# A Mamba-2 block between two FFNs: the out projection from rounded halves, with the loop's weight halves made on GpSimd

## The chip, the cores and the metric

One NeuronCore of a Trainium2 chip runs the whole kernel. The metric is the device time of one execution in microseconds, lower is better. The engines are PE (TensorE), DVE (VectorE), ACT (ScalarE), POOL (GpSimd) and SP (SyncE, which here only issues DMAs). Each runs its own instructions in order; semaphores join them.

## What is computed

The input is x, 2048 tokens by 256 channels, float32. Layernorm and half an FFN are added, then a Mamba-2 mixer on the layernorm of that, then half an FFN again. The mixer, cut to what matters:

```python
proj = hidden_states @ in_proj_w           # gate (4096), x, B, C, dt
hbc = silu(conv4(proj_xBC) + conv_b)       # causal, 4 taps, per channel
dt = softplus(dt + dt_bias); dA = dt * -exp(A_log); cum = cumsum(dA, chunk)
scores = (C @ B.T) * exp(cum_i - cum_j) * dt_j          # j <= i
Y_diag = scores @ x
states = sum_l exp(cum_end - cum_l) * dt_l * B_l x_l
new = exp(cum_end) * prev + states         # scan over chunks, prev starts at 0
Y_off = (C @ prev) * exp(cum)
hidden = (Y_diag + Y_off + D * x) * silu(gate)
hidden = hidden * rsqrt(mean(hidden**2) + EPS) * norm_w
out = hidden @ out_proj_w                  # 4096 -> 256
```

There are 64 heads of 64 channels and a state of 128 per head. The kernel uses chunks of 128 tokens in place of the reference's 32, which gives the same sums.

## The kernel before

**Stages.** The prologue decodes the FFN weights, runs the first FFN in 24 ticks (`for k in range(FFN_TICKS)`) and, beside it and in the first eight slots of the loop, makes B, C, dt and the decay tables (`prep`). Then comes the mixer's loop, then the second FFN. The changed work stands in the loop, and its first weights in `prep` of the FFN's ticks.

**The loop.** The 64 heads are 32 pairs (a pair is 128 channels), taken in 8 groups of GP = 4 pairs; the 2048 tokens are NT = 4 tiles of 512. A piece of work v is one pair of one tile. In a group of SLOTS = 16 pieces the tile goes slowest: v % 4 is the pair, v // 4 % 4 the tile t. Each engine runs `for s in range(-8, 128)`; slot s handles different pieces in different stages, and u below is s % 16.

- PE in slot s: states(s+2), turn_x(s+3), diag(s+1), proj_g(s+8), proj_x(s+8), out_proj(s), off(s+2). The two projections are six products each of rounded halves (`split_matmul`: high x high, high x low, low x high, for two blocks of 128 rows); out_proj is two plain float32 products (128 x 128 weights, 512 columns), each two records in the trace. off is four float32 products, one a chunk, with the state before that chunk as the stationary side; for t = 0 the first state is `zero_state`, a tile of zeros.
- DVE in slot s: conv_tap(s+7) in three steps, with scan(s+2) of one chunk between them (two instructions a chunk, one per head), times_dt and to_chunk_end(s+3), the fourth scan, skip_path(s+1) (adds D*x, writes `hid`), masked(s+2) (the decay times CB, 128 x 1024, both operands in SBUF), scale_off(s+2) (the off products times `e_row`, 512 columns), and in slots with s % 4 == 3 add_out(s).
- ACT in slot s: square(s), relus(s+3) (eight pieces of exp's argument), evac_g and evac_x(s+8), exps(s+3). In slots with s % 4 == 0 the silus of four pieces, seven of the eight before relus, come first, and the evacuations and the eighth silu too. The weight work stands at the end of a slot: `split_g_hi` at u = 6 and 8, `split_x_hi` at u = 6 to 9, `scale_wo` at u = 13 to 15 and 0.
- POOL in slot s: add_squares(s), sum_halos(s+8) in some, gate(s+1) (`hid` times silu of the gate), then `split_g_lo` at u = 6 and 8 and `split_x_lo` at u = 6 to 9.
- SP in slot s: load_cum(s+5), load_e(s+4), then weight loads of the next group. load_cum(v) waits for relus(v-2), load_e(v) for scale_off(v-2). `e_row` has two buffers. Each is a row of 512 read for 128 or 64 partitions from DRAM, two loads a piece.

**What the order hangs on.** out_proj(v) waits for gate(v) and the scaled weights. proj_g(v) waits for the gate weights of its half of the group (`gw_lo_done`, pair_of(v)//2 + 1), proj_x(v) for its pair's. off(v) waits for the scans and for skip_path(v-1), which frees the PSUM bank. scale_off(v) waits for off(v) and `e_row`, diag(v) for scale_off(v). skip_path(v) waits for diag(v) and, since `hid` has two buffers, for out_proj(v-2). ACT's square(v) waits for gate(v) and for add_squares(v-1).

## Time and profile before

| | us |
|---|---|
| median of 3 runs (1499.59 to 1504.02) | 1502.01 |
| profiled execution, its own time | 1504.3 |
| its span, first to last instruction | 1502.2 |
| mean granted TensorE clock | 0.968 of full |
| PE, DVE, ACT, POOL busy | 1384.0, 1182.2, 1037.0, 547.7 |
| loop in its regular part | about 354 to 1317 us |

The trace is that of one execution. A busy time counts an instruction from its start to its end; matmuls of a stream overlap, so that the distance between two starts, and not the busy time of one, is what a product costs. In the timeline instructions of one line that follow each other are merged, with their count. A timeline row has the start in us, the busy time in us, engine, line, operation, tiles written and read with their sizes, and the count. The bracket at the end of a row is the idle time of that engine before it and whom it waited for. SPq is the queue of SP's DMA issues; the view of one tile gives, for the DMA issues in a stretch, the shortest, median and longest time from issue to landing. The loop's rows stand from the third group of pairs, whose slot u = 1 starts its projections at 614.03; the seven groups repeat to 0.02 us.

### The profile page before, as it was taken

How to read it: one execution, taken by the hardware profiler on the slowest of the kernel's cores; microseconds unless marked ns; L12 is line 12 of the kernel's file. 1: busy time of each engine (PE TensorE's matmuls, PEld its weight loads, DVE VectorE, ACT ScalarE, POOL GpSimd, SP SyncE). 2: the span in 40 equal slices, each digit the busy share in tenths (PEclk: the TensorE clock that was granted, in tenths of full speed). 3: DMA queues.
4: the chain of work that ended last, by engine and by line, in shares of the span. 5: the costliest groups of instructions: out<-in, count | busy, mean ns of one | idle time of the engine just before them, and what ended most of it. 6: DMA issues, size and time to landing. Idle time of an engine off the chain costs nothing. (4 is left out here: it accounts for less than half of the span.)

```text
span 1502.2 us, 26126 instructions
## 1 busy us (share of the span) xinstructions
PE 1384.0 (92%) x8704; PEld 1087.0 (72%) x8704; DVE 1182.2 (79%) x2675; ACT 1037.0 (69%) x2133; POOL 547.7 (36%) x511
## 2 busy tenths in 40 slices
PE   5889977777999999999999999999999999986998
PEld 4878766555777777777777777777777777764787
DVE  5753443675999999999999999999999999996433
ACT  1124433666898888889888888988888898871332
POOL 1003211013444454445445444544544454451000
PEclk9999989888999999999999999999999999996999
DMA  5220000223434444343454534545433444324000
GB/s 125 72 88 25 15 15 14 63 50 92 117 96 108 123 111 116 101 109 104 110 130 105 114 99 103 117 112 121 114 104 92 117 118 109 97 88 182 15 14 28
DMA packets 102078, 136.35 MB, mean 91 GB/s; under 512 B 27744, under 2 KB 49856, under 8 KB 101824
## 3 DMA queue, kind: packets, MB, share of 16 engines
q1 hardware_dynamic: 99840, 132.67, 33.8%
q10 hardware_dynamic: 2112, 2.10, 0.4%
q8 instruction: 68, 1.11, 0.3%
q14 instruction: 58, 0.48, 0.1%
HBM read 124.76 MB, written 9.96 MB: 90 GB/s over the span
## 5 line engine op out<-in xcount | busy, mean ns | idle before, releaser
L998 POOL TENSOR_TENSOR hid<-hid,sg 128x512 f32<-128x512 f32 x128 | 272.7, 2130 | 372.8 <-DVE hid L1265 371.0
L844 ACT ACTIVATE M<-cum_row,cum_table 128x128 f32<-128x128 f32 x1024 | 312.0, 390 | 0.0
L1203 DVE SCALAR_TENSOR_TENSOR xs<-psum,conv_w_sb,xs 128x509 f32<-128x509 f32 (+2 forms) x384 | 285.1, 742 | 0.4
L1598 PE MATMUL psum<-hid,wo 128*128 128x512 f32 x512 | 243.1, 597 | 9.6 <-ACT eT L755 9.3
L987 POOL TENSOR_TENSOR squares<-squares,sq 128x512 f32<-128x512 f32 x124 | 165.9, 1338 | 158.9 <-ACT sq L821 158.6
L1230 DVE TENSOR_TENSOR M<-M,CB 128x1024 f32<-128x1024 f32 x128 | 158.7, 1240 | 0.0
L1598 PEld LDWEIGHTS psum<-hid,wo 128*128 128x128 f32 x512 | 96.2, 189 | 84.6 <-issue 72.9
L1257 DVE TENSOR_TENSOR psum<-psum,e_row 128x512 f32<-128x512 f32 x128 | 89.5, 699 | 81.5 <-PE psum L1572 81.5
L1583 PE MATMUL psum<-M,xdt 128*64 128x128 f32 x2048 | 140.1, 279 | 0.9 <-DVE psum L1257 0.9
L1558 PE MATMUL psum<-xend,B_tok 128*128 128x128 f32 x1024 | 137.2, 278 | 0.0
L852 ACT ACTIVATE M<-M 128x1024 f32<-128x1024 f32 x128 | 134.5, 1051 | 0.5
L821 ACT ACTIVATE sq<-hid 128x512 f32<-128x512 f32 x124 | 77.5, 625 | 78.8 <-POOL hid L998 78.8
L858 ACT ACTIVATE xs<-psum,conv_b_sb,conv_w_sb 128x512 f32<-128x512 f32 x128 | 98.6, 770 | 46.0 <-PE psum L40 46.0
L1558 PEld LDWEIGHTS psum<-xend,B_tok 128*128 128x128 f32 x1024 | 127.1, 195 | 1.1 <-issue 1.0
L1583 PEld LDWEIGHTS psum<-M,xdt 128*64 128x64 f32 x2048 | 109.2, 136 | 22.3 <-issue 22.2
L1250 DVE SCALAR_TENSOR_TENSOR inner<-inner,decay_table,psum 128x64 f32<-128x64 f32 x512 | 118.5, 275 | 0.0
L38 PE MATMUL psum<-xT_hi,gw_hi 128*128 128x512 f32 x256 | 114.6, 448 | 2.2 <-DVE x_res L1061 1.5
L1572 PE MATMUL psum<-CT,inner 128*128 128x128 f32 x768 | 107.9, 277 | 0.0
L826 ACT ACTIVATE sg<-psum 128x512 f32<-128x512 f32 x128 | 74.7, 583 | 45.7 <-PE psum L40 38.0
L40 PE MATMUL psum<-xT_hi,gw_lo 128*128 128x512 f32 x256 | 102.1, 399 | 0.0
L38 PE MATMUL psum<-xT_hi,xw_hi 128*128 128x512 f32 x256 | 101.6, 397 | 0.0
L39 PE MATMUL psum<-xT_lo,gw_hi 128*128 128x512 f32 x256 | 101.5, 396 | 0.0
(201 smaller groups left out, 2912.4 us busy)
## 6 DMA issues: line engine op xcount, KB each, us to landing
cum_row<-cum_scratch SPq DMA_DIRECT2D x256, 256.0 KB, 4.3
e_row<-e_scratch SPq DMA_DIRECT2D x256, 128.0 KB, 3.6
xw_raw<-L_attn_in_proj_w_dram SPq DMA_DIRECT2D x32, 128.0 KB, 2.9
wo_raw<-L_attn_out_proj_w_dram SPq DMA_DIRECT2D x32, 128.0 KB, 3.0
gw_raw<-L_attn_in_proj_w_dram SPq DMA_DIRECT2D x16, 256.0 KB, 6.6
x_res<-_attn_hidden_states_dram ACTq DMA_DIRECT2D x4, 512.0 KB, 9.8
x_scratch<-x_res SPq DMA_DIRECT2D x4, 512.0 KB, 2.6
x_res<-x_scratch SPq DMA_DIRECT2D x1, 2048.0 KB, 8.8
```

The lines of the kernel that those rows point to most:

```text
L38: nc.tensor.matmul(out, l_hi, r_hi, start=start, stop=False, skip_group_check=skip)
L844: last = nc.scalar.activation(M[:, v % 3, h, c * CH:(c + 1) * CH], cum_row[:, v % 2, h, c * CH:(c + 1) * CH], ACT.Relu, bias=scalar_of(CUM ...
L852: nc.scalar.activation(M[:, v % 3], M[:, v % 3], ACT.Exp, scale=-1.0).then_inc(exp_done, 1)
L987: nc.gpsimd.tensor_tensor(squares[:, tile(t)], squares[:, tile(t)], sq[:], ALU.add).then_inc(squares_done, 1)
L998: nc.gpsimd.tensor_tensor(hid[:, v % 2, :], hid[:, v % 2, :], sg[:, v % 8, :], ALU.mult).then_inc(hid_done, 1)
L1203: nc.vector.scalar_tensor_tensor(xs[:, v % 8, shift:], psum[:, X_BANK + v % 2, 0:TT - shift], tap_of(v, step), xs[:, v % 8, shift:], ALU.m ...
L1230: nc.vector.tensor_tensor(M[:, v % 3], M[:, v % 3], cb, ALU.mult).then_inc(M_done, 1)
L1250: nc.vector.scalar_tensor_tensor(after, before, scalar_of(CHUNK_DECAY, v, chunk, h), psum[:, ST_BANK, c * P + h * HP:c * P + (h + 1) * HP] ...
L1558: last = nc.tensor.matmul(psum[:, ST_BANK, c * P:(c + 1) * P], B_tok[:, t * CPT + c, :], xend[:, v % 2, c].rearrange("p h q -> p (h q)"), ...
L1572: last = nc.tensor.matmul(psum[:, Y_BANK, c * CH:(c + 1) * CH], before.rearrange("p h q -> p (h q)"), CT[:, tok:tok + CH], start=(c == 0), ...
L1583: last = nc.tensor.matmul(psum[h * HP:(h + 1) * HP, Y_BANK, c * CH:(c + 1) * CH], xdt[:, v % 3, c, h, :], M[:, v % 3, h, c * CH:(c + 1) * CH],
L1598: last = nc.tensor.matmul(psum[:, OUT_BANK + m, :], wo[:, j, m * P:(m + 1) * P], hid[:, v % 2, :], start=(j == 0), stop=(j == GP - 1))
```

## The change

1. **Out projection.** `wo` (float32) becomes `wo_hi` and `wo_lo`, `hid` gets `hid_hi` (two buffers) and `hid_lo` (one). out_proj is now 2 x 3 products of rounded halves. POOL makes the halves of the product in `split_hid(s+1)`, right behind gate(s+1).
2. **Loop weights on POOL.** `split_x` (u = 5, 6, 7, 9), `split_g` (u = 6, 9) and `split_wo` (u = 13, 14, 15 and 1 of the next group) make the high halves by a copy and the low ones by a subtraction, all on POOL; ACT's part in the loop goes. Before the loop ACT still makes high halves, in ticks moved about.
3. **Zero state.** For t = 0, off skips the first chunk, scale_off leaves out its columns, and scan of the first chunk is one copy. `zero_state` goes.
4. **Room.** `e_row`, `xend` go from two buffers to one, `xdt` from three to two, `gw_raw` to half a group's gate weights; load_e moves from s+4 to s+3 and waits for scale_off(v-1), loads are moved to fit.

The diff, cut to its core:

```diff
@@ tiles @@
-    wo = sb("wo", [P, GP, D], F32)
+    wo_hi = sb("wo_hi", [P, GP, D], F32R)
+    wo_lo = sb("wo_lo", [P, GP, D], F32R)
-    e_row = sb("e_row", [P, 2, TT], F32)
-    xdt = sb("xdt", [P, 3, CPT, 2, HP], F32)
-    xend = sb("xend", [P, 2, CPT, 2, HP], F32)
+    e_row = sb("e_row", [P, TT], F32)
+    xdt = sb("xdt", [P, 2, CPT, 2, HP], F32)
+    xend = sb("xend", [P, CPT, 2, HP], F32)
+    hid_hi = sb("hid_hi", [P, 2, TT], F32R)
+    hid_lo = sb("hid_lo", [P, TT], F32R)
+    G_TICKS = (4, 7)
+    WO_TICKS = (5, 6, 12, 15)
+    X_SLOTS = (5, 6, 7, 9)
+    G_SLOTS = (6, 9)
@@ sync @@
             def load_e(v):
-                sp.wait_ge(off_scaled, nth(v - 2))
+                sp.wait_ge(off_scaled, nth(v - 1))
...
-                if alive(s + 4):
-                    load_e(s + 4)
+                if alive(s + 3):
+                    load_e(s + 3)
...
                 if u == 4:
                     load_g_weights(2 * (g + 1))
+                if u == 7:
                     load_g_weights(2 * (g + 1) + 1)
-                if u in (7, 8):
-                    load_x_weights((g + 1) * GP + u - 5)
+                if u in (6, 7):
+                    load_x_weights((g + 1) * GP + u - 4)
-                if u in (13, 14):
-                    load_wo((g + 1) * GP + u - 11)
+                if u in (14, 15):
+                    load_wo((g + 1) * GP + u - 12)
@@ scalar, in the loop @@
-                if g < GROUPS - 1 and u in (6, 8):
-                    split_g_hi(2 * (g + 1) + u // 2 - 3)
-                if g < GROUPS - 1 and 6 <= u < 6 + GP:
-                    split_x_hi((g + 1) * GP + u - 6)
-                if g < GROUPS - 1 and u >= 13:
-                    scale_wo((g + 1) * GP + u - 13)
-                if g > 0 and u == 0:
-                    scale_wo(g * GP + GP - 1)
@@ gpsimd @@
+            def split_hid(v):
+                pool.wait_ge(hid_done, nth(v))
+                pool.wait_ge(out_done, nth(v - 2))
...
+                nc.gpsimd.tensor_copy(hid_hi[:, v % 2, :], hid[:, v % 2, :]).then_inc(hid_hi_done, 1)
+                pool.wait_ge(hid_hi_done, nth(v))
+                pool.wait_ge(out_done, nth(v - 1))
+                nc.gpsimd.tensor_tensor(hid_lo[:], hid[:, v % 2, :], hid_hi[:, v % 2, :].bitcast(F32),
+                                        ALU.subtract).then_inc(hid_lo_done, 1)
+            def split_x(p):
+                cols = slice(p % GP * P, (p % GP + 1) * P)
+                pool.wait_ge(xw_in[p % 2], (p // 2 + 1) * 16)
+                pool.wait_ge(x_proj, nth(last_of(p - GP)))
+                nc.gpsimd.tensor_copy(xw_hi[:, :, cols], xw_raw[:, p % 2]).then_inc(xw_hi_done, 1)
+                split_x_lo(p)
+            def split_g(q):
+                cols = slice(q % 2 * 2 * P, (q % 2 + 1) * 2 * P)
+                pool.wait_ge(gw_in, (q + 1) * 16)
+                pool.wait_ge(g_proj, nth(last_of(2 * q + 1 - GP)))
+                nc.gpsimd.tensor_copy(gw_hi[:, :, cols], gw_raw[:]).then_inc(gw_hi_done, 1)
+                split_g_lo(q)
+            def split_wo(p):
+                pool.wait_ge(wo_in[p % 2], (p // 2 + 1) * 16)
+                nc.gpsimd.tensor_tensor(wo_raw[:, p % 2, :], wo_raw[:, p % 2, :], norm_sb[:, p:p + 1].to_broadcast([P, D]),
+                                        ALU.mult).then_inc(wo_done, 1)
+                pool.wait_ge(out_done, nth(last_of(p - GP)))
+                pool.wait_ge(wo_done, p + 1)
+                nc.gpsimd.tensor_copy(wo_hi[:, p % GP, :], wo_raw[:, p % 2, :]).then_inc(wo_hi_done, 1)
+                split_wo_lo(p)
...
                 if alive(s + 1):
                     gate(s + 1)
+                    split_hid(s + 1)
                 g, u = divmod(s, SLOTS)
+                if g > 0 and u == 1:
+                    split_wo(g * GP + GP - 1)
                 if s < 0 or g == GROUPS - 1:
                     continue
+                if u in X_SLOTS:
+                    split_x((g + 1) * GP + X_SLOTS.index(u))
+                if u in G_SLOTS:
+                    split_g(2 * (g + 1) + G_SLOTS.index(u))
+                if u >= 13:
+                    split_wo((g + 1) * GP + u - 13)
@@ vector @@
+                if chunk == 0:
+                    nc.vector.tensor_copy(inner[:, v % 2, 0].rearrange("p h q -> p (h q)"),
+                                          psum[:, ST_BANK, 0:P]).then_inc(scan_step, 1)
+                    return
...
+                cols = slice(CH if at_slot(v)[1] == 0 else 0, TT)
+                nc.vector.tensor_tensor(psum[:, Y_BANK, cols], psum[:, Y_BANK, cols], e_row[:, cols],
+                                        ALU.mult).then_inc(off_scaled, 1)
...
             def skip_path(v):
-                dve.wait_ge(out_done, nth(v - 2))
+                dve.wait_ge(hid_lo_done, nth(v - 2))
@@ tensor @@
             def off(v):
-                for c in range(CPT):
+                first = 1 if t == 0 else 0
+                for c in range(first, CPT):
...
             def out_proj(v):
-                pe.wait_ge(hid_done, nth(v))
-                pe.wait_ge(wo_done, pair_of(v) + 1)
+                pe.wait_ge(hid_hi_done, nth(v))
+                pe.wait_ge(hid_lo_done, nth(v))
+                pe.wait_ge(wo_lo_done, pair_of(v) + 1)
...
-                    last = nc.tensor.matmul(psum[:, OUT_BANK + m, :], wo[:, j, m * P:(m + 1) * P], hid[:, v % 2, :],
-                                            start=(j == 0), stop=(j == GP - 1))
+                    last = split_matmul(nc, psum[:, OUT_BANK + m, :], wo_hi[:, j, cols], wo_lo[:, j, cols],
+                                        hid_hi[:, v % 2, :], hid_lo[:], start=(j == 0), stop=(j == GP - 1))
```

## Rows read from the trace of the kernel before

**Rows 1.** Page, part 1: busy us, share of span, instructions.
```profile
PE 1384.0 (92%) x8704; PEld 1087.0 (72%) x8704; DVE 1182.2 (79%) x2675; ACT 1037.0 (69%) x2133; POOL 547.7 (36%) x511
```

**Rows 2.** Timeline, PE, first projection: u=1, u=10, next u=1.
```profile
614.03 0.50 PE L38 MATMUL psum<-xT_hi,gw_hi 128*128 128x512 f32 x1
...
687.09 0.50 PE L38 MATMUL psum<-xT_hi,gw_hi 128*128 128x512 f32 x1
...
743.80 0.50 PE L38 MATMUL psum<-xT_hi,gw_hi 128*128 128x512 f32 x1
```

**Rows 3.** Timeline, PE, slot u = 14: projections, out projection, off.
```profile
719.96 0.39 PE L38 MATMUL psum<-xT_hi,gw_hi 128*128 128x512 f32 x1
...
722.06 1.88 PE L1598 MATMUL psum<-hid,wo 128*128 128x512 f32 x4
...
723.77 0.38 PE L1572 MATMUL psum<-CT,zero_state 128*128 128x128 f32 x2
...
723.99 0.83 PE L1572 MATMUL psum<-CT,inner 128*128 128x128 f32 x6
```

**Rows 4.** Timeline, DVE, POOL, PE, scale_off of u=3 to u=4.
```profile
635.63 0.70 DVE L1257 TENSOR_TENSOR psum<-psum,e_row 128x512 f32<-128x512 f32 x1 [0.57 <-PE psum L1572]
...
636.24 1.28 DVE L1278 TENSOR_TENSOR mixed<-psum,mixed 128x512 f32<-128x512 f32 x2
...
637.43 0.15 DVE L1195 COPY halo<-psum 128x3 f32<-128x3 f32 x1
...
641.94 0.47 DVE L1250 SCALAR_TENSOR_TENSOR carry<-inner,decay_table,psum 128x64 f32<-128x64 f32 x2
...
642.32 0.75 DVE L1265 SCALAR_TENSOR_TENSOR hid<-xs,d_sb,psum 128x512 f32<-128x512 f32 x1
...
642.98 1.23 DVE L1230 TENSOR_TENSOR M<-M,CB 128x1024 f32<-128x1024 f32 x1
...
643.15 2.19 POOL L998 TENSOR_TENSOR hid<-hid,sg 128x512 f32<-128x512 f32 x1 [3.58 <-DVE hid L1265]
...
643.21 0.46 PE L1572 MATMUL psum<-CT,carry 128*128 128x128 f32 x2 [0.57 <-DVE hid L1265]
...
644.38 0.70 DVE L1257 TENSOR_TENSOR psum<-psum,e_row 128x512 f32<-128x512 f32 x1 [0.18 <-PE psum L1572]
```

**Rows 5.** POOL groups by form: busy us, mean ns; idle before.
```profile
L959 POOL TENSOR_TENSOR gw_lo<-gw_raw,gw_hi 128x512 fp32r<-128x512 f32 x14 | 18.0, 1282 | 24.9 <-ACT gw_hi L694 24.9
...
L953 POOL TENSOR_TENSOR xw_lo<-xw_raw,xw_hi 128x256 fp32r<-128x256 f32 x28 | 20.5, 732 | 0.9
...
L923 POOL MEMSET gate_idx_sb<- 128x256 int32 x1 | 0.3, 312 | 0.3 <-POOLq L1752 0.3
...
L1752 POOL MEMSET const-float32-1.0<- 128x1 f32 x1 | 0.1, 98 | 0.0
```

**Rows 6.** Timeline, POOL and DVE, end of slot u = 9.
```profile
682.65 0.74 POOL L953 TENSOR_TENSOR xw_lo<-xw_raw,xw_hi 128x256 fp32r<-128x256 f32 x1
...
682.92 1.55 DVE L1230 TENSOR_TENSOR M<-M,CB 128x1024 f32<-128x1024 f32 x1
...
683.34 2.27 POOL L987 TENSOR_TENSOR squares<-squares,sq 128x512 f32<-128x512 f32 x1
```

**Rows 7.** Timeline, SP's DMA queue, slot u = 4.
```profile
645.94 0.80 SPq L607 DMA_DIRECT2D cum_row<-cum_scratch  x2
...
646.78 1.09 SPq L615 DMA_DIRECT2D e_row<-e_scratch  x2
```

**Rows 8.** Tile e_row, issues at 614.19 and at 646.78.
```profile
DMA to landing us min/median/max: 4.8/5.1/5.3
...
DMA to landing us min/median/max: 5.8/6.3/6.9
```

**Rows 9.** Timeline, PE, out projection of slot 0.
```profile
346.76 3.75 PE L1598 MATMUL psum<-hid,wo 128*128 128x512 f32 x4 [9.34 <-ACT eT L755]
```

**Rows 10.** Timeline, PE, first off product of slot 120.
```profile
1324.58 0.46 PE L1572 MATMUL psum<-CT,carry 128*128 128x128 f32 x2 [3.29 <-DVE hid L1265]
```

More of the change, by code:

```diff
@@ L401, in macaron @@
     wo_raw = sb("wo_raw", [P, 2, D], F32)
-    wo = sb("wo", [P, GP, D], F32)
+    under, sbu = scope()
+    w_bc_raw = sbu("w_bc_raw", [P, KT, 2 * N], F32)
+    w_dt_raw = sbu("w_dt_raw", [P, KT, H], F32)
+    under.close()
+    wo_hi = sb("wo_hi", [P, GP, D], F32R)
+    wo_lo = sb("wo_lo", [P, GP, D], F32R)
     under, sb = scope()
@@ L505, in scans @@
         g, u = divmod(v, SLOTS)
-        return g * 120 + 8 * u - 2 * max(u - 12, 0) + 2 * c + h + 1
+        t = u // GP
+        earlier = g * (GP * (7 + 8 + 8 + 6)) + 8 * u - min(u, GP) - 2 * max(u - 3 * GP, 0)
+        return earlier + (max(2 * c + h, 1) if t == 0 else 2 * c + h + 1)
     def sums_before(v):
@@ L1247, in scan @@
                     else:
-                        before = zero_state[:, h, :] if t == 0 else carry[:, t % 2, j, h, :]
+                        before = carry[:, t % 2, j, h, :]
                     after = carry[:, (t + 1) % 2, j, h, :] if c == CPT - 1 else inner[:, v % 2, c, h, :]
```

144 lines of the change are left out of this document (78 added, 66 removed).

## The prediction

> **What bounds the kernel now.** I read the page's busy shares first [rows 1]: PE 92%, DVE 79%, ACT 69%, POOL 36%, over prologue, loop and second FFN together. The change touches the loop over 128 slots, so the shares of the loop decide, and more than these the distances between its slots. The first projection of a slot returns every 129.77 us for a group of 16 slots [rows 2]. Inside a group there are only two kinds of slot. Twelve are 7.95 us long and PE runs through them without a gap: six gate and six x products at 0.233 us each (nine of them take 2.10 us), then out_proj from 722.06 to 723.77, 1.71 us, then `off`, states, turn_x, diag [rows 3]. The other four follow add_out (u = 0, 4, 8, 12; u is the slot number modulo 16). There DVE is the bound: from one scale_off to the next it does add_out, three taps, the scans, times_dt, to_chunk_end, skip_path and `masked`, and PE waits 0.57 us for skip_path before `off` [rows 4]. That slot takes 8.75 us (635.63 to 644.38). u = 8 has no halo copy (0.07 less), u = 12 no fourth scan (0.38, 641.94 to 642.32) and no halo product (0.14): 12 x 7.95 + 8.75 + 8.68 + 8.23 + 8.75 = 129.8, which closes with the 129.77 seen. Take add_out's 1.19 us away (636.24 to 637.43) and DVE's own chain is 7.56 us, 0.39 under PE's. So a second bound stands close behind, and what is late on DVE by more than that stays late until the next slot that PE bounds.
>
> **The change, part by part.**
>
> *Out projection.* Now 2 float32 products, four records, 1.71 us [rows 3]. After: 6 rounded products of the projections' form, 6 x 0.233 = 1.40 us. Saved 0.31 us in a slot that PE bounds, which becomes 7.64 us; nothing in the four long ones. The second bound (7.56) is then 0.08 behind.
>
> *Zero state.* In the slots u = 14, 15, 0, 1 the first of four `off` products goes: 0.22 us (723.77 to 723.99) [rows 3]. On DVE two scans at 0.19 us of pitch each (641.94 to 642.32 [rows 4]) become one copy of 128 columns, put at 0.19, and scale_off loses 128 of 512 columns, 0.13 of its 0.70. The three PE-bound ones become 7.42 us, the long one (u = 0) 8.75 - 0.13 - 0.19 - 0.18 = 8.25.
>
> Sum of the direct savings: nine slots x 0.31 + three x 0.53 + 0.50 = 4.88 us a group, 39 us in all, if nothing else moves.
>
> *ACT* loses the loop's weight halves (ten operations a group). It isn't the bound: worth nothing. Before the loop it gets four more copies beside a PE-bound FFN: nothing.
>
> *GpSimd, price of what it gets.* A two-input operation costs 1.28 us for 512 columns, 0.73 for 256 [rows 5]. A one-input copy of such size isn't in the trace. Below, the memset: 0.31 for 256 columns, 0.098 for one, so 0.53 for 512. Above, 1.28, a two-input one. I take 0.62 for 512 and 0.40 for 256, near the memset since it reads one operand at most. [...]
>
> *The halves of the gated product.* Let T be the end of skip_path, where `masked` starts. The gate starts at T + 0.16 and takes 2.19, since `masked` reads at the same time; alone such an operation takes 1.28 [rows 4, 5]. Copy 0.62, a wait on its own semaphore 0.06, subtraction 1.28: done at T + 4.31. The out projection needs it at about T + 6.5, in the next slot. The subtraction also waits for the out projection before; that is over by T + 0.5. add_squares (1.28) is queued behind: GpSimd is free at T + 5.6 of 7.6. Hidden, and ACT's next square that waits for add_squares isn't due before T + 9. Its cover is 2 us; the GpSimd weights use it up.
>
> *The weights on GpSimd.* x: 0.40 + 0.06 + 0.73 = 1.19 us; gate: 0.62 + 0.06 + 1.28 = 1.96; out: 0.73 + 0.06 + 1.19 = 1.98, in one iteration each. One alone fits. The iterations u = 6 and u = 9 have x and gate: GpSimd ends the weights at T + 4.31 + 1.19 + 1.96 = T + 7.46.
> - From u = 9 comes the second gate half. proj_g of slot u = 10 waits for it (pair 2 of the next group). In the trace T of slot 9 is 682.92 [rows 6] and that projection starts at 687.09 [rows 2], T + 4.17; after, T + 3.86. It will find its weights at T + 7.5: PE stands still for 3.6 us. Before, ACT's half was made in slot 8, one slot earlier. Everything behind hangs on this projection (out_proj, off, scale_off), so DVE gains nothing in it either. 3.6 us in each of 7 groups: 25 us.
> - In u = 6, add_squares runs T + 7.46 to 8.75 and the next `masked` comes at T + 7.5. Such a collision is in the trace: the GpSimd subtraction ran from 682.65, `masked` came at 682.92 and took 1.55 instead of 1.22, and the add_squares behind it took 2.27 instead of 1.28 [rows 6]. Each waits for the whole of the other. Between 0 and 1.2 us lost, by a hair's breadth of the start; I take 0.6.
>
> *e_row single.* DVE frees it at the end of scale_off, and the two loads must be there for the next scale_off. SP runs in order: load_cum(s+5) stands ahead of load_e(s+3), and in slots u = 0, 4, 8, 12 its relus are late, behind seven silus. There e_row is issued at 646.78, 2.40 us after scale_off began (644.38), right behind cum_row [rows 4, 7]. The second load starts 0.5 later and lands after another 5.3 us (u = 0), 6.9 (u = 4, with two gate loads behind it) [rows 8]. Now there are two buffers and this has 16 us. After, it lands at 2.40 + 0.31 (ACT's string starts from the gate, which DVE sets, while PE's part comes 0.31 sooner) + 0.5 + 5.4 = 8.6 us after that scale_off, against a slot of 7.64. In u = 1 the string is 0.71 later rather than 0.31 (DVE saves less than PE in the zero slots), landing at 9.0 against 7.42; in u = 5, with one gate load behind instead of two, 6.1 for the last landing and 9.35 in all. So scale_off is late by 1.6 (u = 1), 1.7 (u = 5), 1.0 (u = 9), 1.0 (u = 13). DVE wins back 0.08 to 0.36 a slot until the next DVE-bound slot. Left: 1.5 + 1.4 + 0 (under the 3.6 us stall) + 0.4 = 3.3 us a group.
>
> *xdt at two, xend at one buffer.* They wait for a diag and a states that end 1.6 us or more before: nothing. SP's other loads come in the order in which their buffers free; the nearest, the second gate load, has ten microseconds.
>
> *Ends.* At 346.76 the out projection ran at the low clock, 3.75 us where the loop has 1.88 [rows 3, 9]; six products at twice 0.233 are 2.8 there, and zero products go: -1.5 us. In the last eight slots there are no projections, the slots are some 5.3 us, and GpSimd needs 2.19 + 0.16 + 1.96 + 1.28 = 5.6; the last gate has 1.96 more behind it: +2.5 us.
>
> **Sum.** A group: -4.88 + 3.6 + 0.6 + 3.3 = +2.6 us; seven groups +18.4. The first group's u = 1 has no silus ahead: -1.5. Slots 112 to 119, no weights: -2.6 + 2.1 = -0.5. Ends +1.0. Total +17.4 us. The profiled execution took 1504.3 us, its span 1502.2; the median of the three shown is 1502.0, so the same work varies by 2 us and I count from the median: 1519.4 us, 1.2% slower.
>
> **The rivals.**
> (a) *e_row isn't late.* Its landing was measured among the transfers of now; with one gate load fewer and the loads spread, the tail may fall under 4.4 us. For it: quiet slots. Against: the late ones all have cum_row ahead of e_row, and that stays. Then a group is -4.88 + 3.6 + 0.6 = -0.7, and 1502 - 5 - 2.6 + 1 = 1495.5 us: faster. It decides where e_row lands less than 7.6 us after scale_off began.
> (b) *The full gain.* e_row in time, and the gate half too, if proj_g could run without it: 1502 - 39 + 1 = 1464 us. The wait in the code speaks against it.
> (c) *GpSimd's copy costs as a two-input operation.* Then 0.66 more in each split of the product, and 1.65 in the stall at u = 10 (+11.5 us); with the out weights add_squares ends at T + 8.6 and meets `masked` in four more slots, 2.5 us a group (+17): 1548 us. It decides from a copy of about 0.9 us.
> (d) *The clock falls in the 3.6 us stall.* [...] If 3.6 us is enough, the 4.3 us of projections behind it double: +4 x 7 = 28, 1548 us. [...]
> (e) *The savings are smaller*, the second bound catching all: within the range.
>
> **How the numbers follow.** Forecast 0.55; (a) 0.17; (b) 0.06; (c) 0.13; (d) 0.05; (e) 0.04. Range: the forecast's own terms vary by 0 to 1.2 us in the collision, 1 us in each landing, 0.3 in the stall, some 12 us either way: 1507 to 1532. For 8 in 10 it must take in (a) and half of (c): 1493 to 1545. Faster or slower by over 0.3% (4.5 us, about what a measurement can tell from no change): faster (a), (b) and a sliver, 0.22; same, the edge between (a) and the forecast, 0.14; slower 0.64.
>
> **What would show it.** Out projection: six products, 1.40 us from first to `off`. Stall: PE's first gate projection of u = 10 behind gw_lo on GpSimd, 3 to 4 us, seven times; none refutes it. e_row: DVE's scale_off in u = 1, 5, 9, 13 idle for a DMA, not for PE. Collisions: `masked` over 1.22 us in u = 7. A plain slot 7.64 us, a group 132.4 us. The prediction fails if a group is under 129.8: then (a) or (b); over 134: (c) or (d), told apart by the copy's duration and the granted clock.

## The result, and the profile after

The changed kernel takes 1534.74 us (median of 4 runs, 1534.59 to 1540.67) where the kernel before took 1501.72 in runs beside it: a ratio of 1.0225, 95% interval 1.0208 to 1.0241. It is slower by 33 us, the direction forecast, and within the range; but 17.4 us were forecast. So there is half of the loss to explain as well as its sign.

The page of the changed kernel, part 1 (busy us, share of the span, instructions), and of part 5 the GpSimd groups that are new, by form (busy us, mean ns of one, idle before):

```profile
PE 1351.9 (88%) x8896; PEld 1137.4 (74%) x8896; DVE 1185.1 (77%) x2643; ACT 1011.0 (66%) x2067; POOL 860.0 (56%) x896
```

```profile
L985 POOL TENSOR_TENSOR hid_lo<-hid,hid_hi 128x512 fp32r<-128x512 f32 x128 | 164.3, 1283 | 34.2 <-PE psum L40 24.6
L982 POOL CAST hid_hi<-hid 128x512 fp32r<-128x512 f32 x128 | 78.1, 610 | 9.6 <-DVE ez L1196 1.4
...
L1004 POOL TENSOR_TENSOR wo_raw<-wo_raw,norm_sb 128x256 f32<-128x256 f32 x28 | 17.3, 616 | 0.0
...
L992 POOL CAST xw_hi<-xw_raw 128x256 fp32r<-128x256 f32 x28 | 11.2, 400 | 0.0
```

PE is busy for 32 us less than in [rows 1] and the kernel takes 33 us more: the work left PE as meant, and more than its time came back as waiting. The waits of the regular part (400 to 1300 us; engine and line, whom it waited for, us in all, times, longest) say where:

```profile
DVE psum L1331 <- DMA e_row<-e_scratch: 38.7, 27, 3.3
...
PE psum L1655 <- DVE psum L1331: 24.3, 20, 3.4
...
PE psum L38 <- POOL gw_lo L948: 22.6, 7, 3.6
```

Both waits of the forecast are there: scale_off (L1331) for `e_row` in 27 slots, with `diag` (L1655) behind it, and PE's first gate projection for `gw_lo`, seven times. The sizes stand in the distances from the first projection of a slot to that of the next. Here they are for the third group, beside those of slots without a wait (from the same kernel's quiet slots, and for u = 1 and u = 10 from later runs):

```
u            1     2     3     4     5     6     7     8     9     10    11    12    13    14    15    0      sum
after        8.50  7.93  7.61  8.75  8.49  7.86  7.61  8.69  12.49 9.09  7.59  8.23  7.63  7.52  7.39  8.22   133.6
no wait      7.39  7.60  7.60  8.75  7.61  7.60  7.60  8.68  7.60  7.60  7.60  8.24  7.60  7.38  7.38  8.20   124.4
```

The seven groups last 132.4 to 135.3, mean 133.4, against 129.77 before [rows 2]. The rows without a wait give the direct savings: a plain slot 7.60 (forecast 7.64), one of tile 0 7.38 (7.42), u = 0 8.21 (8.25). The rest, 9 us a group, is in three places: u = 1, 2, 5, 6 (the single `e_row`), the distance 12.49 in column 9 (the stall, with the projection of u = 10 at its end) and the slot behind it, 9.09.

The chain into that stall, from iteration u = 6 on, in the timeline of the changed kernel (GpSimd, ACT, SP's queue, DVE and PE; start, busy us, idle before in the bracket):

```profile
668.66 0.61 POOL L999 CAST gw_hi<-gw_raw 128x512 fp32r<-128x512 f32 x1
...
669.35 1.30 POOL L948 TENSOR_TENSOR gw_lo<-gw_raw,gw_hi 128x512 fp32r<-128x512 f32 x1
...
670.61 2.39 POOL L1049 TENSOR_TENSOR squares<-squares,sq 128x512 f32<-128x512 f32 x1
...
670.64 1.22 DVE L1299 TENSOR_TENSOR M<-M,CB 128x1024 f32<-128x1024 f32 x1
...
672.96 1.28 POOL L1060 TENSOR_TENSOR hid<-hid,sg 128x512 f32<-128x512 f32 x1
...
674.27 0.63 ACT L822 ACTIVATE sq<-hid 128x512 f32<-128x512 f32 x1 [2.66 <-POOL hid L1060]
...
680.85 0.70 DVE L1331 TENSOR_TENSOR psum<-psum,e_row 128x512 f32<-128x512 f32 x1 [0.18 <-PE psum L1644]
...
681.54 2.44 ACT L845 ACTIVATE M<-cum_row,cum_table 128x128 f32<-128x128 f32 x8
...
684.00 0.81 SPq L613 DMA_DIRECT2D cum_row<-cum_scratch  x2
...
684.86 1.09 SPq L621 DMA_DIRECT2D e_row<-e_scratch  x2
...
686.88 1.22 DVE L1299 TENSOR_TENSOR M<-M,CB 128x1024 f32<-128x1024 f32 x1
...
686.95 2.28 POOL L1049 TENSOR_TENSOR squares<-squares,sq 128x512 f32<-128x512 f32 x1 [3.10 <-ACT sq L822]
...
689.18 1.26 POOL L1060 TENSOR_TENSOR hid<-hid,sg 128x512 f32<-128x512 f32 x1
...
690.27 0.70 DVE L1331 TENSOR_TENSOR psum<-psum,e_row 128x512 f32<-128x512 f32 x1 [2.18 <-DMA e_row<-e_scratch]
...
694.27 1.27 POOL L948 TENSOR_TENSOR gw_lo<-gw_raw,gw_hi 128x512 fp32r<-128x512 f32 x1
...
695.59 0.79 PE L38 MATMUL psum<-xT_hi,gw_hi 128*128 128x512 f32 x1 [3.38 <-POOL gw_lo L948]
```

In iteration 6 the x and gate weights end at 670.65, the sum of squares behind them coincides with `masked` (670.64) and takes 2.39 in place of 1.28 us; `masked` keeps its 1.22. The gate stands behind the sum, so ACT's square comes at 674.27 after 2.66 us of idling, and with it the silus, relus (681.54), cum_row (684.00) and `e_row` (684.86, 4.01 us after the scale_off of 680.85; [rows 4, 7] had 2.40). scale_off then waits 2.18 for `e_row`. ACT's next square is late by the same string, so in iteration 9 the next sum lies on top of `masked` again (686.95 and 686.88), and gw_lo, seven operations behind it, ends at 695.54, T + 8.66 with T = 686.88. Behind the stall the granted clock is 0.50 for some 3 us, in the view by stretches (columns: length, PE, PEld, DVE, ACT, POOL busy with their instructions, granted clock, DMA share, GB/s):

```profile
695.60:697.00 1.40, 1.40 (x3) 1.15 (x4) 1.40 (x2) 0.00 (x0) 1.40 (x2) 0.50 0.84 187
697.00:698.40 1.40, 1.40 (x5) 1.07 (x4) 0.85 (x1) 0.00 (x0) 1.40 (x1) 0.50 0.71 138
698.40:700.00 1.60, 1.60 (x8) 1.29 (x7) 0.00 (x0) 0.60 (x1) 1.20 (x2) 0.86 0.06 12
700.00:702.00 2.00, 2.00 (x13) 1.74 (x12) 0.00 (x0) 1.85 (x3) 0.35 (x1) 1.00 0.01 4
```

The twelve projections take 4.36 us (695.59 to 699.95, where the out projection starts) in place of 2.89 (683.10 to 685.99, one slot earlier).

### The profile page after: what moved, and what is told of

Same layout as the page of the kernel before. It is cut to its first block and busy times, and to the rows that moved or that the text cites. A ratio compares the mean times of both kernels' runs of the same rounds, so it can differ in the third digit from the quotient of the medians.

```text
span 1532.9 us, 27111 instructions
## 1 busy us (share of the span) xinstructions
PE 1351.9 (88%) x8896; PEld 1137.4 (74%) x8896; DVE 1185.1 (77%) x2643; ACT 1011.0 (66%) x2067; POOL 860.0 (56%) x896
## 5 line engine op out<-in xcount | busy, mean ns | idle before, releaser
L1060 POOL TENSOR_TENSOR hid<-hid,sg 128x512 f32<-128x512 f32 x128 | 261.0, 2039 | 170.4 <-DVE hid L1340 164.8
L1049 POOL TENSOR_TENSOR squares<-squares,sq 128x512 f32<-128x512 f32 x124 | 176.1, 1420 | 62.7 <-ACT sq L822 62.7
L985 POOL TENSOR_TENSOR hid_lo<-hid,hid_hi 128x512 fp32r<-128x512 f32 x128 | 164.3, 1283 | 34.2 <-PE psum L40 24.6
L1299 DVE TENSOR_TENSOR M<-M,CB 128x1024 f32<-128x1024 f32 x128 | 171.0, 1336 | 0.0
L1331 DVE TENSOR_TENSOR psum<-psum,e_row 128x512 f32<-128x512 f32 (+1 forms) x128 | 85.2, 666 | 108.9 <-PE psum L1644 67.2
L1655 PE MATMUL psum<-M,xdt 128*64 128x128 f32 x2048 | 140.7, 279 | 26.2 <-DVE psum L1331 26.1
L1655 PEld LDWEIGHTS psum<-M,xdt 128*64 128x64 f32 x2048 | 110.5, 137 | 48.7 <-issue 48.7
L38 PE MATMUL psum<-xT_hi,gw_hi 128*128 128x512 f32 x256 | 118.5, 463 | 24.8 <-POOL gw_lo L948 22.6
L936 POOL TENSOR_TENSOR ffn_hidden_lo<-ffn_hidden,ffn_hidden_hi 128x512 fp32r<-128x512 f32 x24 | 30.8, 1282 | 179.6 <-ACT ffn_hidden_hi L677 179.6
L38 PE MATMUL psum<-hid_hi,wo_hi 128*128 128x512 f32 x256 | 101.7, 397 | 17.3 <-ACT eT L756 9.4
L1644 PEld LDWEIGHTS psum<-CT,inner 128*128 128x128 f32 x768 | 98.4, 194 | 12.3 <-DVE carry L1323 7.8
L40 PE MATMUL psum<-xT_hi,gw_lo 128*128 128x512 f32 x256 | 105.3, 411 | 0.0
```

Source lines behind the costliest of these rows:

```text
L38: nc.tensor.matmul(out, l_hi, r_hi, start=start, stop=False, skip_group_check=skip)
L40: return nc.tensor.matmul(out, l_lo, r_hi, start=False, stop=stop, skip_group_check=skip)
L985: nc.gpsimd.tensor_tensor(hid_lo[:], hid[:, v % 2, :], hid_hi[:, v % 2, :].bitcast(F32), ALU.subtract).then_inc(hid_lo_done, 1)
L1049: nc.gpsimd.tensor_tensor(squares[:, tile(t)], squares[:, tile(t)], sq[:], ALU.add).then_inc(squares_done, 1)
L1060: nc.gpsimd.tensor_tensor(hid[:, v % 2, :], hid[:, v % 2, :], sg[:, v % 8, :], ALU.mult).then_inc(hid_done, 1)
L1299: nc.vector.tensor_tensor(M[:, v % 3], M[:, v % 3], cb, ALU.mult).then_inc(M_done, 1)
```

## The experiments

All ratios are against runs of the kernel before on the same chip (medians 1501.4 to 1501.8 us).

**One `e_row` in the kernel before.** The single buffer alone, with its load one slot later.

```diff
-                sp.wait_ge(off_scaled, nth(v - 2))
+                sp.wait_ge(off_scaled, nth(v - 1))
-                if alive(s + 4):
-                    load_e(s + 4)
+                if alive(s + 3):
+                    load_e(s + 3)
...
-                dve.wait_ge(e_in[v % 2], (v // 2 + 1) * 32)
+                dve.wait_ge(e_in[0], (v + 1) * 32)
```

> The kernel before with one e_row buffer in use: load_e(s+3), waiting for scale_off(v-1); nothing else is changed. Theory A (the single buffer costs in the slots behind the silus, since load_e stands behind load_cum on SP): the second load of the trace lands 2.40 + 0.5 + 5.4 = 8.3 us after scale_off began against a slot of 7.95, and 9.8 in u = 5 with two gate loads behind it. DVE has 0.39 us a slot to win back, so only u = 5 leaves something, about 1 us a group: +6 to +12 us, 1508 to 1514 us, and DVE waits for e_row's DMA in u = 1, 5, 9, 13. Rival B (the loads hurt only together with a late GpSimd): same time within 3 us, no wait of DVE for e_row.

Measured: 1504.84 us, ratio 1.0019 (1.0007 to 1.0031), a group 130.0 to 130.3. That is under theory A's range and 3.4 us above the kernel before, so just outside rival B's 3 us too. The wait is there:

```profile
DVE psum L1257 <- DMA e_row<-e_scratch: 13.9, 14, 1.6
```

Fourteen waits, two a group: 1.3 to 1.6 us in u = 5 and some 0.5 in u = 9. What is left of them is 0.4 us a group, where about 1 was expected. The landing hits a slot of 7.95 us in which DVE, with its chain of 7.56, has 0.39 us to make good; in the changed kernel the slot is 7.60 and DVE has next to none, and the same buffer costs 2.4 us a group. So the price of the single buffer depends on the saving it was bought for.

**Second gate half one iteration earlier.** In the changed kernel:

```diff
-    G_SLOTS = (6, 9)
+    G_SLOTS = (6, 8)
```

> The changed kernel with the second gate half split on GpSimd in slot u = 8 instead of u = 9. Theory A (the late gate half holds PE at u = 10, and the clock falls behind it): the wait of PE for gw_lo goes, PE's granted clock stays whole, the distance of 12.5 us from u = 9 to u = 10 falls to what e_row allows, about 9, and u = 10 to 7.6. That is 5 us in each of seven groups: 1500 us, 1495 to 1506. Rival B (GpSimd is late as such, and the wait only moves to another consumer): 1525 to 1535 us, with the waits on hid_lo or xw_lo in its place.

Measured: 1496.53 us, ratio 0.9968 (0.9955 to 0.9981). One number takes 38 us off and makes the change a gain. The wait for gw_lo is gone, u = 10 takes 7.61 us, u = 9 8.8 to 9.0 (9.4 in the last group). The waits that are left:

```profile
DVE psum L1331 <- DMA e_row<-e_scratch: 35.5, 28, 2.5
```

Twenty-eight waits, four a group: under the stall the `e_row` of u = 9 was hidden, and now leaves 1.2 to 1.4 us (1.8 in the last). 12.49 + 9.09 - 8.9 - 7.61 = 5.1 us a group, seven times 36.

**`e_row` ahead of cum_row.** In the changed kernel SP issues load_e first, then load_cum.

```diff
-                if alive(s + 5):
-                    load_cum(s + 5)
                 if alive(s + 3):
                     load_e(s + 3)
+                if alive(s + 5):
+                    load_cum(s + 5)
```

> The changed kernel with load_e(s+3) ahead of load_cum(s+5) on SP, so that e_row no longer waits behind cum_row, which waits for late relus. Theory A: e_row is issued 0.7 us after scale_off begins and lands within 5 us; DVE's wait for it (about 40 us in the loop) goes. u = 1, 2, 5, 6 give 2.3 us a group and slot 113 its 4 us; u = 9 keeps the gate's wait, which partly covers its own: 1534.7 - 16 - 4 = 1515, 1508 to 1520 us. Rival B (cum_row becomes late instead, since it now waits for scale_off): ACT waits for cum_row, 1530 us or more.

Measured: 1525.69 us, ratio 1.0158 (1.0141 to 1.0175): 9 us gained where 20 were expected, outside theory A's range and under rival B's. The wait for `e_row` is gone from the list (u = 1 is 7.39, u = 5 7.6), so the order on SP was its cause. But the groups still take 132.8 in the mean, against 133.4:

```profile
PE psum L38 <- POOL gw_lo L948: 33.8, 7, 4.8
```

The stall grew from 3.4 to 4.8 us: the distance to the projection of u = 10 stays 12.49, since GpSimd's string in iteration 9 does not come earlier when scale_off does, and PE only reaches the unfinished gw_lo sooner. Behind the longer stall the clock stays low for longer: in the third group it is 0.50 in the whole stretch from 693.56 to 699.00, and u = 10 takes 10.2 us in place of 9.09 (9.8 to 10.4 over the groups), 1.0 us more in the mean. And u = 2 is 8.62 us. So the two losses aren't added; each covers the other in part. Of the 9 us, 4.0 are in the seven groups and 4.4 in the six slots behind them.

**Both.**

```diff
-    G_SLOTS = (6, 9)
+    G_SLOTS = (6, 8)
-                if alive(s + 5):
-                    load_cum(s + 5)
                 if alive(s + 3):
                     load_e(s + 3)
+                if alive(s + 5):
+                    load_cum(s + 5)
```

> Both edits together. Theory A (these two and the clock are all that is lost): a group falls from 133.2 to the direct savings, 124.9, within 0.7 us; 1534.7 - 58 - 4 = 1473 us, 1468 to 1480, under the kernel before. Rival B (GpSimd's load itself costs by collisions with masked): some 1.5 us a group more, 1484 us or above.

Measured: 1479.76 us, ratio 0.9858 (0.9841 to 0.9874), 22 us faster than the kernel before. A group is 126.25 us (the first 125.2); neither of the two waits is in the list any more. The 1.8 us over 124.4 stand in u = 2 (8.63) and u = 10 (8.38), the slots whose conv waits for ACT behind its seven silus:

```profile
DVE halo L1264 <- ACT xs L859: 12.8, 14, 1.3
```

**The high halves on ACT again.** The version before, with the high halves of all loop weights in ACT's loop as in the kernel before (the changed slots kept), and the low ones on GpSimd.

```diff
@@ scalar, in the loop @@
+                if g < GROUPS - 1 and u in G_SLOTS:
+                    split_g_hi(2 * (g + 1) + G_SLOTS.index(u))
+                if g < GROUPS - 1 and u in X_SLOTS:
+                    split_x_hi((g + 1) * GP + X_SLOTS.index(u))
+                if g < GROUPS - 1 and u >= 13:
+                    scale_wo((g + 1) * GP + u - 13)
+                if g > 0 and u == 0:
+                    scale_wo(g * GP + GP - 1)
@@ gpsimd, in the loop @@
-                    split_x((g + 1) * GP + X_SLOTS.index(u))
+                    split_x_lo((g + 1) * GP + X_SLOTS.index(u))
-                    split_g(2 * (g + 1) + G_SLOTS.index(u))
+                    split_g_lo(2 * (g + 1) + G_SLOTS.index(u))
```

> The kernel of run e4 with the weights' high halves made on ACT in the loop again (slots 5, 6, 7, 9 for x, 6 and 8 for the gate, 13 to 16 for the out weights); GpSimd keeps the low halves. Theory A (GpSimd's place for the halves is worth little now, either engine can carry them): 1476 to 1484 us, within 0.3% of e4. Rival B (GpSimd's load is what still delays gates in e4): the extra 1 us in u = 2 and 0.8 in u = 10 go, 1466 to 1472 us. Rival C (ACT is too full, the move off it bought the gain): over 1488 us.

Measured: 1485.5 us, ratio 0.99 (0.9882 to 0.9918), 6 us more than on GpSimd, between theory A's range and rival C's. ACT now waits for the raw weights in front of its own work, and u = 2 becomes 9.4 to 9.8 us in five groups and 11.35 in one:

```profile
ACT xw_hi L692 <- DMA xw_raw<-L_attn_in_proj_w_dram: 8.6, 7, 1.8
ACT wo_raw L710 <- DMA wo_raw<-L_attn_out_proj_w_dram: 7.3, 7, 1.8
```

The second part of the change, counted at nothing on ACT in the prediction, is worth some 6 us once nothing else is late, with the loads placed as they are here. In u = 10 it is the other way round: that slot falls from 8.38 to 7.6 to 8.0 us in six of the seven groups, so part of its lateness did come from the high halves on GpSimd.

**Plain products in the out projection.** The version with both edits, with two float32 products on `hid` and wo_hi; the low halves are made but not used, so that the weights' low parts are missing in the out projection.

```diff
-                    last = split_matmul(nc, psum[:, OUT_BANK + m, :], wo_hi[:, j, cols], wo_lo[:, j, cols],
-                                        hid_hi[:, v % 2, :], hid_lo[:], start=(j == 0), stop=(j == GP - 1))
+                    last = nc.tensor.matmul(psum[:, OUT_BANK + m, :], wo_hi[:, j, cols].bitcast(F32), hid[:, v % 2, :],
+                                            start=(j == 0), stop=(j == GP - 1))
```

> The kernel of run e4 with the out projection as two plain float32 products again, on the product itself and on the high halves of the out weights (their low halves are made, but not used, so the output is a little off). All copies, subtractions and waits on GpSimd stay. Theory A (the six products save 0.31 us in each slot that PE bounds): plain slots go from 7.61 to 7.92 us, zero slots from 7.38 to 7.69, a group from 126.25 to about 129.6: 1480 + 3.4 x 7.5 = 1505 us, 1500 to 1510. Rival B (DVE bounds these slots now): under 1490 us.

Measured: 1495.97 us, ratio 0.9964 (0.995 to 0.9978), a group 128.55. Plain slots are 7.95 in place of 7.60, those of tile 0 7.72 in place of 7.38: the six products save 0.34 us in each of twelve slots, 4.1 us a group. But the whole is 16 us, 2.3 a group, and not the 25 expected (the time lies between the two ranges), since in the longer slots the lateness of u = 2 and u = 10 has gone (7.94 each): 4.1 - 1.8 = 2.3.

**The gate ahead of the sum of squares.** Same version; in slots with s % 4 == 1 GpSimd does gate(s+1) before add_squares(s), so that the sum can't hold it up.

```diff
+                if alive(s) and s % GP == 1:
+                    gate(s + 1)
...
-                    gate(s + 1)
+                    if s % GP != 1 or s < 0:
+                        gate(s + 1)
```

> The kernel of run e4 with gate(s+1) ahead of add_squares(s) on GpSimd in slots s % 4 == 1. Theory A (in the slot behind ACT's silus the square is late, add_squares then runs into masked and holds the gate behind it, and ACT's evacuation comes late for DVE in u = 2 and u = 10): masked takes 1.22 us in u = 1 again, u = 2 falls from 8.62 to 7.6 and u = 10 from 8.38 to 7.6: 1.8 us a group, 1466 us, 1463 to 1471. Rival B (squares then come late for ACT, and ACT is as late as before): 1478 us or more.

Measured: 1485.48 us, ratio 0.9895 (0.9878 to 0.9911), where 1466 was expected: theory A is refuted, rival B's 1478 or more holds. u = 2 and u = 10 stay at 8.73 and 8.37, and u = 0 gets worse (8.65). The lateness in u = 2 isn't made on GpSimd. ACT's rows of the last experiment show it: it works without a gap from the silus on (below).

**PE kept busy through the stall.** In the changed kernel, 14 products of an x weight block go into the gate's PSUM bank ahead of the wait for gw_lo, in the pieces with v % 16 = 2, whose gate projection stands in slot u = 10; the projection overwrites them. PE's wait for that bank (`g_evac`) moves ahead of them.

```diff
+                pe.wait_ge(g_evac, nth(v - 1))
+                if v >= SLOTS and v % SLOTS == 2:
+                    for _ in range(14):
+                        nc.tensor.matmul(bank(G_BANK), xw_hi[:, 0, 0:P], xT_hi[:, 0, 0:TT], start=True, stop=True)
                 pe.wait_ge(gw_lo_done, pair_of(v) // 2 + 1)
-                pe.wait_ge(g_evac, nth(v - 1))
```

> The changed kernel with 14 extra products (3.3 us, written to the gate's bank and overwritten) ahead of PE's wait for the late gate half, once in each of seven groups. PE is busy where it stood still; nothing comes earlier. Theory A (the stall of 3.4 us also halves the clock for the projections behind it, 4.36 us instead of 2.8): the granted clock stays whole behind the stall, the distance from u = 10 to u = 11 falls from 9.1 to 7.6 us: 1534.7 - 10 = 1524 us, 1521 to 1528. Rival B (the long records there come from the late weights, not from the clock): 1535 us within 3.

Measured: 1522.44 us, ratio 1.0143 (1.0126 to 1.016). The projection comes no earlier (the distance is 12.5), the granted clock is 1.00 from it on, and the slot behind it is whole:

```profile
690.97 0.50 PE L38 MATMUL psum<-xT_hi,gw_hi 128*128 128x512 f32 x1 [0.16 <-POOL gw_lo L948]
...
698.59 0.50 PE L38 MATMUL psum<-xT_hi,gw_hi 128*128 128x512 f32 x1
```

7.62 us in place of 9.09, 1.5 us in this group and 11 in the seven, of 12.3 us gained. That is what the fallen clock cost.

**The zero state alone.** The kernel before with part 3 only (no zero products, 384 columns in scale_off for tile 0, one copy in the first scan).

```diff
+                if chunk == 0:
+                    nc.vector.tensor_copy(inner[:, v % 2, 0].rearrange("p h q -> p (h q)"),
+                                          psum[:, ST_BANK, 0:P]).then_inc(scan_step, 1)
+                    return
...
-                nc.vector.tensor_tensor(bank(Y_BANK), bank(Y_BANK), e_row[:, v % 2, :], ALU.mult).then_inc(off_scaled, 1)
+                cols = slice(CH if at_slot(v)[1] == 0 else 0, TT)
+                nc.vector.tensor_tensor(psum[:, Y_BANK, cols], psum[:, Y_BANK, cols], e_row[:, v % 2, cols],
+                                        ALU.mult).then_inc(off_scaled, 1)
...
-                for c in range(CPT):
+                first = 1 if t == 0 else 0
+                for c in range(first, CPT):
```

> The kernel before with the third part of the change alone: for tile 0 off skips the first chunk, scale_off leaves out its 128 columns, the first scan is one copy. All buffers, loads and the out projection stay as before. Theory: the prediction's zero state step, alone. Three plain slots of tile 0 become 0.22 us shorter (7.95 to 7.73) and the slot u = 0 about 0.4 to 0.5 us, so 1.1 to 1.2 us a group, 9 us in all: 1492.5 us (1489.5 to 1495). Rival: in the slots of tile 0 PE waits for scale_off or the scans anyway, and the time stays within 3 us of the kernel before (1498 to 1503).

Measured: 1492.78 us, ratio 0.9933 (0.9914 to 0.9952): 9.0 us faster, as expected; slots of tile 0 7.72 and 8.21.

**The x weights out of the crowded iteration.** In the changed kernel:

```diff
-    X_SLOTS = (5, 6, 7, 9)
+    X_SLOTS = (5, 7, 8, 9)
...
-                if u in (6, 7):
-                    load_x_weights((g + 1) * GP + u - 4)
+                if u in (7, 8):
+                    load_x_weights((g + 1) * GP + u - 5)
```

> The changed kernel with one edit: the x weights' halves of pairs 1 and 2 are made in the iterations u = 7 and 8 in place of u = 6 and 7 (and their raw weights loaded a slot later), so that the iteration u = 6 holds the gate weights' halves alone and the x and gate weights no longer stand in one iteration there. Theory A: in the changed kernel the squares' sum of iteration 7 starts at the same time as masked, takes 2.39 in place of 1.28 us and holds the gate back; from there ACT's square and silus, relus, the two row loads and scale_off of u = 10 are late, and the second half of the gate weights ends 1.2 us later than forecast. With 1.1 us less in iteration 6 the sum ends before masked, ACT's square comes about 2 us earlier, gw_lo ends 1 us or more earlier, PE's idle time at the first projection of u = 10 falls from 3.4 us to 2.5 or less and with it the half clock behind it goes: group 133.4 to 131, 1516 us (1508 to 1524). Rival B: the load's landing or scale_off's own wait sets the end, whatever the gate does: the stall stays over 3.2 us, 1530 to 1538 us. Rival C: the x halves now in iteration 8 push the gate of iteration 9 late by as much: 1525 to 1535 with the gate late in iteration 9 instead.

Measured: 1528.9 us (1525.69 to 1531.65), ratio 1.0183 (1.0157 to 1.0208). The time is outside theory A's range, a little under rival B's and inside rival C's, but C's sign, a late gate in iteration 9, isn't there: it starts 0.16 us after `masked`, on time. The timeline, iteration 9 again (GpSimd, SP's queue, DVE, PE):

```profile
680.14 1.09 SPq L621 DMA_DIRECT2D e_row<-e_scratch  x2
...
682.22 1.30 POOL L1049 TENSOR_TENSOR squares<-squares,sq 128x512 f32<-128x512 f32 x1 [0.70 <-ACT sq L822]
...
683.38 1.22 DVE L1299 TENSOR_TENSOR M<-M,CB 128x1024 f32<-128x1024 f32 x1
683.54 2.19 POOL L1060 TENSOR_TENSOR hid<-hid,sg 128x512 f32<-128x512 f32 x1
...
685.73 0.70 DVE L1331 TENSOR_TENSOR psum<-psum,e_row 128x512 f32<-128x512 f32 x1 [1.12 <-DMA e_row<-e_scratch]
...
689.55 1.27 POOL L948 TENSOR_TENSOR gw_lo<-gw_raw,gw_hi 128x512 fp32r<-128x512 f32 x1
...
690.88 0.50 PE L38 MATMUL psum<-xT_hi,gw_hi 128*128 128x512 f32 x1 [3.21 <-POOL gw_lo L948]
```

The mechanism of theory A is there: the sum of squares stands ahead of `masked` and takes 1.30, gw_lo ends at 690.82, T + 7.44 (T = 683.38), 1.22 us earlier against T, and the distance to that projection is 11.27 in place of 12.49 in all seven groups. What A got wrong is PE's pause: scale_off's wait for `e_row` shrank by 1.06 as well, so PE reaches the projection earlier too and still stands 3.21 us (2.98 to 3.57 over the groups), and the clock still falls:

```profile
692.30:693.70 1.40, 1.40 (x5) 1.03 (x4) 0.85 (x1) 0.60 (x1) 1.40 (x1) 0.50 0.83 117
```

The slot behind takes 8.9 to 9.2 again, once 10.3. 1.22 x 7 = 8.5 us from the distance, and the groups together are 10.9 us shorter in the profiled execution; the medians differ by 5.8, with 6 us between this kernel's own runs.

**The same on the best version.** `e_row` first, gate weights in iterations 6 and 8, x weights in 5, 7, 9 and 10.

```diff
-    X_SLOTS = (5, 6, 7, 9)
-    G_SLOTS = (6, 9)
+    X_SLOTS = (5, 7, 9, 10)
+    G_SLOTS = (6, 8)
```

> The version with the second half of the gate weights in iteration u = 8 and load_e ahead of load_cum (1479.76 us), with the x weights' halves in the iterations u = 5, 7, 9 and 10 in place of 5, 6, 7 and 9, so that no iteration holds both x and gate weights. Theory A: what is left of the loss in u = 10 (8.38 us in place of 7.6) comes from the crowded iteration 6 or 8, through a late gate, ACT's square and the evacuations: it goes, 0.8 us a group, 1474 us (1470 to 1477). Rival B: it is ACT's own silu slot together with the row loads, the same as in u = 2, where no weights are made: 1478 to 1482 us.

Measured: 1478.26 us (1476.05 to 1479.23), ratio 0.9842 (0.9823 to 0.986). u = 10 falls from 8.38 to 8.04, u = 2 stays at 8.62, a group is 125.9. The time is in rival B's range. So somewhat under half of the 0.8 us in u = 10 came from the crowded iteration; the rest and u = 2 did not. The gain over 1479.76 is within what the two intervals leave open. ACT in slot u = 1 of this version:

```profile
599.05 2.44 ACT L845 ACTIVATE M<-cum_row,cum_table 128x128 f32<-128x128 f32 x8
...
601.50 1.28 ACT L853 ACT_TABLE_LOAD   x1
...
602.80 1.06 ACT L853 ACTIVATE M<-M 128x1024 f32<-128x1024 f32 x1
...
603.76 0.61 ACT L822 ACTIVATE sq<-hid 128x512 f32<-128x512 f32 x1
...
604.28 2.44 ACT L845 ACTIVATE M<-cum_row,cum_table 128x128 f32<-128x128 f32 x8
...
606.62 0.58 ACT L827 ACTIVATE sg<-psum 128x512 f32<-128x512 f32 x1
...
607.10 0.77 ACT L859 ACTIVATE xs<-psum,conv_b_sb,conv_w_sb 128x512 f32<-128x512 f32 x1
...
607.90 0.16 DVE L1264 COPY halo<-psum 128x3 f32<-128x3 f32 x1 [0.59 <-ACT xs L859]
```

No row has an idle bracket, nor has one of the rows between the square before the silus (591.78) and these: ACT is full from the silus to evac_x, and DVE's conv waits for it. So with the slots at 7.60 us ACT's silu string looks like the next bound. That this is the whole of the last 1.5 us a group was not tested by a run that shortens the string.

## Why the prediction was right, and where its sizes failed

- **Out projection and zero state.** Right: 7.60, 7.38 and 8.21 us against 7.64, 7.42 and 8.25, and 9.0 us for the zero state alone. Together they save 5.3 us a group rather than 4.88: 0.04 more in nearly every slot (the products save 0.34, not 0.31).
- **GpSimd's prices.** Right: 0.610 and 0.400 us for the copies, taken at 0.62 and 0.40. Rival (c) needed 0.9 and is out. One term was too high: the multiplication by the norm's weights takes 0.616 us, not 0.73; nothing depended on it. The halves of the product were hidden, as said.
- **The gate half in iteration 9.** The mechanism and the place were right: PE's first gate projection of u = 10 behind gw_lo, seven times. Its size was T + 7.46 and 3.6 us; the changed kernel had T + 8.66 and 4.89 (12.49 - 7.60). The run that clears iteration 6 has T + 7.44 and 11.27 - 7.60 = 3.67: the forecast's number for a GpSimd that starts its iteration on time. The missing term, 1.22 us a group, is the delay inherited from iteration 6. That PE's pause there, 3.38 us, looks like the forecast's 3.6 is chance: another 1.39 us of the lateness had already gone by in the wait of `diag` for scale_off.
- **The collision in iteration 6.** This is the step that failed. I priced it on DVE, at 0 to 1.2 us, took 0.6, and called it a loss of `masked`. `masked` kept its 1.22 us; the sum of squares lost. From there it went to the gate behind it and to ACT's square, silus and relus, and then two ways at once: by ACT's next square to the sum and the weights of iteration 9, which end 1.22 us later against T and push the projection of u = 10 by as much, 8.5 us in all; and by SP's two loads to scale_off, which made PE's pause shorter and the projection no later (with `e_row` first the distance stays 12.49). The prediction held that ACT's next square "isn't due before T + 9" and didn't ask what stands behind it in a silu slot. In these rows, of two that overlap one takes longer by most of what is left of the other: the sum began within 0.1 us of `masked` and took 2.39 and 2.28 us, not far under 1.22 + 1.28, while `masked` took 1.22 both times. In [rows 6], where a subtraction had begun 0.27 us earlier, `masked` was the one that took longer, 1.55, so 0.33 more with 0.47 of the subtraction left, and the sum behind it took 0.99 more with 1.13 of `masked` left. So "the whole of the other" in the prediction put it a little high. Which of two that start together gives way they do not settle: at 670.61 the sum has the earlier start, by 0.03 us, and lost.
- **e_row.** Forecast 3.3 us a group, and in the first group 1.5 less, so 3.1 in the mean; measured 2.4 in the mean, and nothing in u = 1 of the first group, as forecast: u = 1 and 2 1.1 + 0.3, u = 5 and 6 0.9 + 0.3 in this group (less in others), u = 13 and 14 under 0.2. (The landing in u = 5, given as 9.35, adds up to 9.31.) The cause was as said (load_cum ahead of it on SP: with the order turned it goes). Rival (a), not late, is out. The forecast made the single buffer and the shorter slot two separate terms; the first run shows that alone it costs 0.4, so most of the loss comes from the single buffer and the shorter slot together.
- **Rival (d), the clock.** It had 0.05 and came true, for some two fifths of its price. Behind the 9.34 us of idle before 346.76 the trace has the granted clock at 0.50 and the out projection at 3.75 us, twice the 1.88 of the loop [rows 3, 9]. The mistake in the price was to double all 4.3 us of the projections: in the trace the twelve last 2.89 us at full clock (1.00), and 4.36 behind the stall, because the clock is back before the last of them (0.86 in the mean from 698.40 to 700.00). 1.5 us x 7 = 10.5 us, and 12.3 in the run that keeps PE busy. The mistake in the chance was a misread row. I had taken from [rows 10] that the clock did not fall behind the 3.29 us of idle before 1324.58. The two records there are short, but the view by stretches of the same trace (columns as above) has the clock at 0.50 within half a microsecond, and the next six `off` products take 1.45 us where they have 0.83 in [rows 3]:

```profile
1324.58:1325.10 0.52, 0.52 (x4) 0.52 (x5) 0.52 (x1) 0.52 (x3) 0.52 (x1) 0.83 0.00 0
1325.10:1326.50 1.40, 1.40 (x8) 1.40 (x8) 0.61 (x2) 1.38 (x5) 1.40 (x1) 0.50 0.00 0
```

```profile
1324.88 1.45 PE L1572 MATMUL psum<-CT,inner 128*128 128x128 f32 x6
```

  So the row that was used against (d) spoke for it.
- **The ends.** Start -2.0 (forecast -1.5). Slots 112 to 119: +3.5 where -0.5 was forecast, since scale_off of u = 1 (slot 113) waited 3.30 us and the clock fell behind it as well (0.55 in the mean from 1296 to 1298 us). From the last projection to the second FFN's first load +4.9, forecast +2.5: without projections GpSimd's string sets the slot, 5.71 us from gate to gate where the kernel before has 5.30.

```profile
1364.18 2.19 POOL L1060 TENSOR_TENSOR hid<-hid,sg 128x512 f32<-128x512 f32 x1 [0.25 <-DVE hid L1340]
...
1369.88 2.18 POOL L1060 TENSOR_TENSOR hid<-hid,sg 128x512 f32<-128x512 f32 x1 [0.23 <-DVE hid L1340]
```

The account of what the forecast was low by, measured less forecast. In a group: savings -0.4, stall +1.3, collision on DVE -0.6, clock +1.6, e_row -0.7 (against the 3.1), which is 1.2, seven times 8.2 us. The last group +4.0, the drain +2.4, the start -0.5, and 0.7 less behind the loop's end, where nothing was forecast. That is 13.4 us, against 13.3 between the 30.7 us by which the spans of the profiled executions differ and the 17.4 forecast; the medians are 33.0 apart, 2.3 more.

So the direction was right for the reasons given, and a number near the right one would have needed two terms that it had in hand as a 0.6 and as a rival of 0.05. That the time lies in the stated range is in part luck: the forecast's own terms gave 1507 to 1532, which 1534.74 misses, and the upper end had been put out to 1545 for rival (c), the dear copy, which did not come. The term that was too high, `e_row`, hid a part of those that were too low.

## What to carry to other kernels

When work goes to an engine with room, look for the iteration in which two of its new jobs meet, and follow the delay past that engine: here 1.1 us of conflict between GpSimd and DVE in iteration 6 reached PE three slots later, by way of ACT. Buffers given up to pay for a speed-up have to be costed at the new, shorter slot and not at the old one. And a change that measures slower may be one constant from a gain: the same work, with one job moved one iteration earlier and two loads exchanged, is 1.4% faster than the kernel before instead of 2.2% slower, so test the placement before the idea is dropped. And whether a pause costs the clock is to be read from the granted clock some microseconds behind it (here 0.50 from 1325.10 to 1326.50, behind the pause that ended at 1324.58), and not from the first records (here 0.46 us for two, the short length).
